# Attention and routed feed-forward on one Trainium2 core: the four parts of a key stored next to each other, on chip and in memory, with new order tables

## What is computed

```python
x = x + tanh(g_xattn) * attention(layernorm(x), ctx)      # 16 heads of 16 features, keys and values from ctx
x = x + tanh(g_ffn) * ffn(layernorm(x))

def attention(x, y):
    q, k, v = x @ wq + bq, y @ wk + bk, y @ wv + bv        # each split into 16 heads
    attn = softmax(q @ k.T / sqrt(16))
    return (attn @ v) @ wo + bo

def ffn(x):
    top1 = argmax(softmax(x @ gate_w.T))                   # one of 2 experts for each token
    routing = sum over e of (relu(masked_e @ w1[e] + b1[e]) @ w2[e] + b2[e])
    shared = relu(x @ sw1 + sb1) @ sw2 + sb2
    return routing + shared
```

## Time and profile before

| what | us |
|---|---|
| time, median of 3 runs | 333.23 |
| lowest, highest | 333.08, 334.18 |
| the profiled execution, its own time | 334.0 |
| its span, first to last instruction | 332.2 |
| PE busy | 317.3 (96%) |
| PEld busy | 281.9 (85%) |
| DVE busy | 229.9 (69%) |
| ACT busy | 214.7 (65%) |
| POOL busy | 177.5 (53%) |
| mean granted TensorE clock | 0.998 of full speed |

### The profile page before, as it was taken

The page is one execution under the profiler, slowest core; times in us unless marked ns, Lnnn a source line. Parts: engine busy times, 40 slices in busy tenths (PEclk is TensorE's granted clock), DMA queues, the critical chain, the costliest instruction groups (busy, mean ns, idle before and its releaser), DMA issues.

```text
span 332.2 us, 7324 instructions
## 1 busy us (share of the span) xinstructions
PE 317.3 (96%) x2383; PEld 281.9 (85%) x2383; DVE 229.9 (69%) x517; ACT 214.7 (65%) x483; POOL 177.5 (53%) x261
## 2 busy tenths in 40 slices
PE   7998889999999999999999999989899999999993
PEld 7776767779887878887988889979899999999992
DVE  6899989997697997896537649943445455454473
ACT  3757999679958655879493865536547555564652
POOL 6266997835755086449340577512536535544552
PEclk9999999999999999999999999999999999999999
DMA  7877844731017044101006501444524511222200
GB/s 196 271 239 207 224 95 105 214 94 13 3 16 216 2 104 118 67 13 66 0 2 201 180 32 63 151 123 175 190 98 155 205 47 65 80 63 66 78 32 28
DMA packets 38151, 35.69 MB, mean 107 GB/s; under 512 B 16608, under 2 KB 35060, under 8 KB 37613
## 3 DMA queue, kind: packets, MB, share of 16 engines
q1 hardware_dynamic: 34568, 27.36, 28.1%
q0 software_dynamic: 2720, 7.32, 6.8%
q10 hardware_dynamic: 837, 0.67, 0.7%
HBM read 21.20 MB, written 9.85 MB: 93 GB/s over the span
## 4 chain that ended last, share of the span: by engine, by line
PE 60%; issue 11%; POOL 7%; DMA 7%; DVE 6%; SPq 4%; ACT 3%; POOLq 1%; ACTq 0%; DVEq 0%
PE y_ps L1545 20%; PE h_ps L1545 14%; PE s_ps L1545 10%; PE bank L1545 9%; PE bank L1678 4%; POOL sorted_dram L710 2%; DMA stage<-in_ctx 2%; DMA sorted_dram<-empty_rows 2%; SPq L482 1%; POOL hT_lo L719 1%; DVE smax L1249 1%; DMA part_dram<-x_all 1%; PE bank L1782 1%; DVE rsum L1267 1%; DMA part<-part_dram,gather_token 1%
## 5 line engine op out<-in xcount | busy, mean ns | idle before, releaser
L693 POOL TENSOR_TENSOR probs<-probs,rinv 128x616 f32<-128x616 f32 x32 | 40.8, 1287 | 34.4 <-DVE rinv L1271 34.4
L1545 PE MATMUL y_ps<-sw,hT_hi 128*128 128x256 f32 x272 | 57.8, 292 | 1.1 <-DVE hT_lo L1523 0.7
L1545 PE MATMUL y_ps<-ew,hT_hi 128*128 128x256 f32 x256 | 54.4, 287 | 1.1 <-DVE hT_lo L1482 1.1
L1482 DVE TENSOR_TENSOR hT_lo<-h,hT_hi 128x256 fp32r<-128x256 f32 x64 | 30.1, 471 | 35.6 <-ACT h L1089 33.8
L1545 PEld LDWEIGHTS y_ps<-sw,hT_hi 128*128 128x128 f32 x272 | 44.9, 190 | 2.5 <-DVE hT_lo L1523 1.7
L1545 PEld LDWEIGHTS y_ps<-ew,hT_hi 128*128 128x128 f32 x256 | 42.6, 188 | 2.4 <-DVE hT_lo L1482 2.4
L1545 PE MATMUL h_ps<-x2T_hi,sw 128*128 128x512 f32 (+1 forms) x160 | 44.0, 362 | 0.0
L1086 ACT ACTIVATE hT_hi<-h_ps,vec_cols 128x256 fp32r<-128x256 f32 x32 | 15.2, 475 | 39.6 <-PE h_ps L1545 32.6
L1545 PE MATMUL y_ps<-sw,hT_lo 128*128 128x256 f32 x136 | 38.3, 282 | 0.0
L1545 PE MATMUL y_ps<-ew,hT_lo 128*128 128x256 f32 x128 | 35.9, 280 | 0.0
L959 ACT ACTIVATE pT<-bank 128x512 f32<-128x512 f32 x40 | 24.2, 623 | 16.3 <-PE bank L1678 16.2
(11 more groups left out here) (208 smaller groups left out, 826.8 us busy)
## 6 DMA issues: line engine op xcount, KB each, us to landing
v_diag<-v_rows SPq DMA_DIRECT2D x16, 256.0 KB
stage<-in_L_ffn_w SPq DMA_DIRECT2D x4, 1024.0 KB, 6.1
sw<-ew SPq DMA_DIRECT2D x4, 1024.0 KB
xs<-sorted_dram SPq DMA_DIRECT2D x8, 257.0 KB, 2.7
stage<-in_L_ffn_sw SPq DMA_DIRECT2D x2, 1024.0 KB, 6.8
x_all<-in_x SPq DMA_DIRECT2D x1, 1536.0 KB, 8.4
part_dram<-x_all SPq DMA_DIRECT2D x3, 512.0 KB, 5.1
k_dram<-probs SPq DMA_DIRECT2D x2, 616.0 KB, 5.4
```

The costliest lines, as they stand in the source:

```text
L693: nc.gpsimd.tensor_tensor(pq, pq, rinv[:, b % 2, k, :].unsqueeze(2).to_broadcast([P, HG, KEYS]), ALU.mult).then_inc(p_ready, 1)
L1482: nc.vector.tensor_tensor(hT[1][:, c % HB, 0:RTOK], h32[:, c % 2, 0:RTOK], hT[0][:, c % HB, 0:RTOK], ALU.subtract).then_inc(h_lo, 1)
L1545: return nc.tensor.matmul(out_, lhsT, rhs, start=start, stop=stop, **kw)
```

## The change

The parts of a key element are made the innermost dimension. In memory `k_dram` was (128, 4 parts, 616) and is (128, 8 batches, 77 keys x 4 parts); on chip `k_own` was [128, 2, 4 parts, 4 heads, 77] and is [128, 2, 4 heads, 77, 4 parts], and `k_parts` likewise ends in the four parts. A row that `keys_in` moves was four runs of 308 bytes and is one run of 1,232 bytes; a row of `keys_out` was four runs of 1,232 bytes and is one of 4,928. ScalarE and GpSimd write every fourth element, and TensorE reads its moving operand from `k_own` with a step of four elements (16 bytes) where it read neighbours. The numbers computed are the same. All five order tables are new.

```diff
@@ the SP table (the others are replaced in the same way)
 SP_ORDER = """
-    kw.0 kw.1 vz.0 vz.1 kr.1 wd.0 vw.0 wd.1 kr.2 vr.0 vw.1 kr.3 vr.1 vw.2 kr.4 wd.3 vr.2 vw.3 vr.3 kr.5 vw.4 kr.6
-    vr.4 wd.2 vw.5 kr.7 vr.5 vw.6 vw.7 vr.6 vr.7 wd.4 wd.5 ps.0 ps.1 xs ps.2 ps.3 fl.0
+    fl.0 kw.0 vz.0 kr.1 vz.1 wd.0 kw.1 vw.0 wd.1 kr.2 vw.1 vr.0 kr.3 vr.1 vw.2 vw.3 vr.2 vr.3 vw.4 kr.4 kr.5 vr.4
+    vw.5 wd.3 vw.6 wd.2 vr.5 kr.6 vr.6 vw.7 kr.7 vr.7 ps.0 ps.1 wd.4 wd.5 ps.2 ps.3 xs
 """
@@ build
-    k_dram = nc.dram_tensor("k_dram", (P, 2 * GROUPS, BATCHES * KEYS), F32).ap()
+    k_dram = nc.dram_tensor("k_dram", (P, BATCHES, KEYS * 2 * GROUPS), F32).ap()
...
-        k_own = sb("k_own", [P, 2, 2 * GROUPS, HH, KEYS], F32R, scope=att)
+        k_own = sb("k_own", [P, 2, HH, KEYS, 2 * GROUPS], F32R, scope=att)
...
-            "p (g n) -> p g n", g=GROUPS)
-        k_parts = probs[:, 1, :, :].rearrange("p q n -> p (q n)").rearrange("p (m g n) -> p m g n", m=2, g=GROUPS)
+            "p (g b k) -> p g b k", g=GROUPS, k=KEYS)
+        k_parts = probs[:, 1, :, :].rearrange("p q n -> p (q n)").rearrange(
+            "p (b k c) -> p b k c", b=BATCHES, k=KEYS)
@@ keys_out
-                cols = slice(half * YH, (half + 1) * YH)
-                sp.dma_start(k_dram[:, :, cols], k_parts[:, :, :, cols].rearrange("p m g n -> p (m g) n")
-                             ).then_inc(k_out[half], 16)
+                batches = slice(half * BATCHES // 2, (half + 1) * BATCHES // 2)
+                sp.dma_start(k_dram[:, batches, :].rearrange("p b n -> p (b n)"),
+                             k_parts[:, batches, :, :].rearrange("p b k c -> p (b k c)")).then_inc(k_out[half], 16)
@@ keys_in
-                    sp.dma_start(k_own[rows, n, :, h % HH, :].bitcast(F32), k_dram[rows, :, b * KEYS:(b + 1) * KEYS]
+                    sp.dma_start(k_own[rows, n, h % HH, :, :].rearrange("p k c -> p (k c)").bitcast(F32), k_dram[rows, b, :]
                                  ).then_inc(k_in[n], 16)
@@ keys_lo
-                nc.gpsimd.tensor_tensor(k_parts[:, 1, g, cols].bitcast(F32R), k32[:, g, cols], k_parts[:, 0, g, cols],
-                                        ALU.subtract).then_inc(k_lo, 1)
+                nc.gpsimd.tensor_tensor(k_parts[:, batches, :, GROUPS + g].bitcast(F32R), k32[:, g, batches, :],
+                                        k_parts[:, batches, :, g], ALU.subtract).then_inc(k_lo, 1)
@@ keys (ScalarE)
-                to = k_parts[:, 0, g, cols].bitcast(F32R) if rounded else k32[:, g, cols]
-                nc.scalar.activation(to, key_bank(half, g), ACT.Copy).then_inc(k_hi if rounded else k_32, 1)
+                to = k_parts[:, batches, :, g].bitcast(F32R) if rounded else k32[:, g, batches, :]
+                nc.scalar.activation(to, key_bank(half, g).rearrange("p (b k) -> p b k", k=KEYS), ACT.Copy).then_inc(k_hi if rounded else k_32, 1)
@@ scores (TensorE)
-                                     k_own[rows, b % 2, km * GROUPS + g, :, :].rearrange("p h k -> p (h k)"), n == 0, n == 2)
+                                     k_own[rows, b % 2, :, :, km * GROUPS + g].rearrange("p h k -> p (h k)"), n == 0, n == 2)
```

98 lines of the change are left out of this document (49 added, 49 removed).

## The result

The changed kernel takes **348.15 us** (median of 4 runs, 346.95 to 350.24) against 333.53 (4 runs): ratio 1.044, 95% interval 1.039 to 1.050, some 14.6 us slower. The forecast was 340.9 with a range that ended at 343.5. The direction was right and the size was not: nearly half of the loss was in no term of the sum.

What follows compares the result with a forecast made beforehand. TensorE was taken to bound the kernel from 70 to 210 us, with no engine full from 30 to 70. Terms 8.0 - 0.6 + 0.3 = 7.7 on 334.0 gave 341.7, less 0.8 for the median: 340.9 us, range 331.8 to 343.5.

Steps and rivals of the forecast that it cites:

- step in the operand: TensorE's score matmuls read keys at half pace: 0.12 us more per pair, 8.0 us together; this case's chance 0.55.
- keys of batch 1 earlier: At the first score of batch 1: keys land sooner, so TensorE starts near 30.75 instead of 31.36, 0.6 us less.
- writing the parts: ScalarE's copies and GpSimd's subtractions before the first store: strided access costs 0 to 1.7 us, counted as nothing.
- late second store: Second store of keys, queued behind the weights, may delay ScalarE's first exponential of batch 1; nothing in the sum.
- rival 1.3: Step free but second store late: ScalarE stands 1.3 us before batch 1's first exponential, 334.2 us; chance 0.21.
- transposes after the last `y`: Passage to the routed part: the last matmuls fill the plan reading, transposes come later, 0.3 us more.
- other moves of the tables: Remaining order moves only exchange neighbours: nothing in the sum, up to 2 us won from TensorE's gaps, 30 to 70 us.
- half of the tight stretch: From 30 to 70 us, 36 score pairs worth 4.3 us extra, of which half, 2.2 us, was counted.
- free: Rival that TensorE's step costs nothing, from a VectorE reduction with a 512-byte step: 332.0 us, chance 0.24.
- long runs would give nothing: Loads of keys: DMA time freed by 2,688 fewer packets was counted at nothing.

Runs made afterwards that it cites:

- e1: Changed layout with all five order tables of the kernel before: 342.95 us, ratio 1.027.
- e16: The changed kernel run again unaltered: 346.41 us, ratio 1.044.
- e3: Changed kernel with the keys' second store moved ahead of the second zeroing and the first load of weights: 345.90 us, ratio 1.037.
- e5: As e4, but a key's high and low parts side by side, so TensorE reads with a step of 8 bytes: 341.57 us, ratio 1.027.
- e7: Kernel before, plus blocks of 12 matmuls with various operand steps at TensorE's end: 382 us, a time that means nothing.
- e2: The five new order tables over the layout of before, with VectorE's store wait moved to quarter 1: 344.18 us, ratio 1.031.
- e6: Kernel before, with the keys' second store moved behind the second zeroing and first weights in SP's queue: 333.65 us, ratio 1.004.
- e10b: Changed kernel with ScalarE's copy of the second group's keys moved ahead by three steps, store left late: 345.79 us, ratio 1.039.
- e14: e11b with the first transposes before the last `y` again and VectorE's 2,048-wide subtraction moved back one step: 342.94 us, ratio 1.032.
- e4: Tables of before; a key's parts together in memory as long runs, but each part's keys packed on chip: 332.76 us, ratio 1.0035.
- e15: Changed kernel with e10b's key copy, e11b's matmul order, the transposes before the last `y` and e14's subtraction move: 345.06 us, ratio 1.041.
- e11b: e3 with TensorE's matmuls `h.4.5` ahead of `y.4.1` again: 346.18 us, ratio 1.039.

## Why the prediction was wrong

| part | forecast | shown |
|---|---|---|
| step in the operand | 8.0 | 9.0 (e1) |
| keys of batch 1 earlier | -0.6 | first score at 30.91 for 31.36, but 31.44 in e16 |
| writing the parts | 0 | 0 at the first score |
| late second store | 0, rival 1.3 | 2.7 by the medians (change against e3); 4.9 and 1.5 in two executions |
| transposes after the last `y` | 0.3 | 0.7 by the wait (1.03 to 1.74) |
| other moves of the tables | 0, to -2 | 3.0, together with the row above and the keys (e3 against e1) |
| whole | 7.7 | 14.6 |

**The step in the operand was read rightly.** The halved pace taken from TensorE's own rows was the right end to choose, the mechanism is as told, and e5 and e7 rule out a price that begins only above 8 bytes. The term was mis-sized by 1.0: 0.12 for a pair was 0.26 - 0.14, where the float32 products were my measure of half pace; the measured price is 0.14, so 84 pairs make 11.8 us in place of 10.1. That half of the tight stretch would be hidden was near, three fifths were. The row that spoke for "free" was a weak witness from the start: that reduction reads PSUM, and the keys lie in the on-chip memory beside it, SBUF. Of the two readings of the rule in the Trainium skill ("SBUF — State Buffer", Door 1: The DMA port swizzle), "4 fp32 for free" is contradicted by 0.28 against 0.14 us. The other, that two hits in each 16-byte line give full bandwidth, falls for TensorE too: at a step of 8 bytes every line has two hits, and the pair still takes 0.28 us (e5).

**Two steps of the sum failed. The first is the second store.** "With slow scores that exponential is later too; I cost it at nothing in the sum and take it up as a rival." Three things in it were wrong. It was made an alternative to the slow scores, though nothing excludes both at once: the change has both. Its landing was bounded by 6.8 us, the longer of the two before, although it now stood behind a megabyte of weights; it took 7.0 to 9.8. And the price ended at the wait itself. A gap of 3.8 us on TensorE was followed by a stretch at 0.66, which the rows show in the change and in e2 (4.58 us), and which they do not show after 1.22 us (e16) or 0.60 us (e6); this was the smallest of the three, at most 0.8 us. In place of nothing it cost 2.7 us by the medians, 4.9 in the profiled execution.

**Why it was late lay only in part in the tables.** Its issue was forecast at about 28.0 and was at 28.97. The first store was issued at 18.40, not by 16.7, since `k32.0.1` had been moved behind three other steps of ScalarE: e2 gives 2.5 us of it (17.47) to the order, and the strided writes add 0.9. I had read SP's table and not ScalarE's. But e10b, which undoes that move, brings the issue forward by only 0.9 us. More of the wait was the landing: 9.8 us in the first profile, 7.7 in e16 at the same place, 7.1 in e10b. What makes it so long, no run here isolates. With the old layout the two moves come apart more clearly: late place alone, issued at 27.61, 0.85 us of wait (e6); with all the tables, issued at 30.77, 4.84 (e2).

**The second failed step is "they only exchange neighbours", together with the tables' end.** The sum had -0.6 + 0.3 for all that the tables do apart from the store, and the runs show 3.0 us. "0.3 more" assumed that the last `y` would fill the time of the reading. What the move did was give up the cover of 0.7 us of matmuls (1.03 to 1.74 us of wait). And "the other moves only exchange neighbours" missed that GpSimd's and VectorE's steps are neighbours too: 0.57 us after VectorE began its 2,048-wide subtraction GpSimd began its own, and it took 2.83 us. The Trainium skill ("SBUF — State Buffer", SBUF: two separate sides) says that the two share a pair of ports, which whoever starts first holds for the whole instruction; GpSimd's 0.77 against 2.83 us in e14 agrees, while VectorE's own 2.83 against 2.28 is more than that sentence asks for. No order table shows such a meeting. Before, such a pair met too, and it fell out the other way: VectorE's record begins at 209.61 and lasts 3.34 us, GpSimd's begins at 210.03 and lasts 0.76. By the durations GpSimd seems to have gone first there, although its record begins later, so the start of a record does not tell who holds the ports.

With the wide subtraction and the transposes put back (e14), the routed part starts at 230.99, and in e1 at 230.92: the tables' 1.8 us up to there are gone. But e14's first score is 0.9 us earlier than e1's (30.6 and 31.5), so the tables still lose about that much in the middle, and the 1.3 us up to the first `y` of the routed part are there as in e3 (13.08 against 11.79).

**The DMA side.** That long runs would give nothing was right, and e4 shows it: 9% fewer packets, ratio 1.0035 with 1 inside the interval.

**What stays open.** The repaired e14 has 1.032 where the layout alone has 1.027, each against its own runs of before; their spans are 340.9 and 340.5. About 1.3 us are in the gap before the first `y` of the routed part; what brings VectorE later there I did not try. Most of e15's 2.1 us over e14 is not traced to a row. Nor is it shown why one store lands after 7.0 us and after 9.8. And in parts of 230 to 250 us the clock is at 0.83 to 0.92 in the change's first profile, e2 and e3, but at 1.00 in e10b, e11b and e16 with the same two gaps. It cost nothing there: from the start of the routed part to its first `y` the change's first profile takes 13.08 us and e3 13.05, with a gap of 0.2 to 0.3 us before that `y`, and e10b 13.00, e11b 13.06 and e16 12.89, with gaps of 1.6 to 1.8. The slower matmuls only filled the wait. What tips it, no run here tells.

## What to carry to other kernels

Lay an operand of TensorE so that neighbouring columns are neighbours on chip; a copy can make the memory side long-run instead, as e4 does, and first ask whether anything waits for those transfers at all. When a whole set of order tables is replaced, follow each late item back through every queue that feeds it, not only the one that it stands in: a step that costs nothing where it stands can hold what is further down. Ask also which steps of two engines will newly meet. And rivals that can happen together with the main case belong in the sum or in the range's outer end, not beside it.

## What was not expected of the hardware

- TensorE's one-pass 4-byte matmul of 308 columns goes from 0.14 to 0.27 us with a step of only 8 bytes, and no further up to 64 bytes; with 2-byte elements 4 bytes are free (0.14), 8 bytes cost 0.27 and 16 bytes 0.54.
- The float32 product, already slower (0.26 us a record), doubles as well (0.54): being slower is no cover.
- ScalarE writes 308 elements in 0.43 us packed, 0.45 with a step of 8 bytes and 0.75 with 16; GpSimd's subtraction takes 0.79 to 0.84, 0.86 and 1.02. So the writers' price sets in at another step than TensorE's.
- The landing of one and the same store, issued at 29.0 and 29.1 us, was 9.8 and 7.7 us in two executions.
- In e7 the granted clock fell to half from 370 us on, though TensorE stood still at no time: what it did before was 2-byte matmuls at a quarter of their pace (0.54 us for 308 columns). The float32 block at 0.54 us a record, from 353.61 to 360.12, had kept 1.00. And the halved clock cost these matmuls nothing: they start 0.54 us apart before the fall and behind it (367.69, 369.32 and 371.50 are three and four matmuls apart). The last 8 us:

```profile
372.00:380.00 8.00, 7.95 (x15) 1.65 (x13) 0.00 (x0) 0.00 (x0) 0.00 (x0) 0.50 0.00 0
```

- A gap of 3.8 us on TensorE was followed by 10 us at 0.66, which are 3.4 us of full-speed work, yet cost at most 0.8. Gaps of up to 1.9 us in e10b to e16 left the clock at 1.00, but gaps of 1.4 and 1.7 us in the change, e2 and e3 were followed by 0.83 to 0.92, which cost nothing.
